# Three edits to a nine-stage layer stack: an unrolled attention stage, experts moved into a gather stage, normalizations spread over three engines

## What is computed

```python
h = h + _L1_attn_ref(_layernorm(h, axis=-1), ...)
h = h + _L1_ffn_ref(_layernorm(h, axis=-1), ...)
...
h = h + _L3_ffn_ref(_layernorm(h, axis=-1), ...)

def _layernorm(x, axis=-1, eps=1e-05):
    m = jnp.mean(x, axis=axis, keepdims=True)
    v = jnp.var(x, axis=axis, keepdims=True)
    return (x - m) / jnp.sqrt(v + eps)
```

```python
a_src = (h * att_src).sum(-1); a_dst = (h * att_dst).sum(-1)
e = jax.nn.leaky_relu(a_src[src] + a_dst[dst], negative_slope=0.2)
... # softmax of e over the edges of each target, weighted sum of h[src]
scores = _layernorm(agg, ln_gamma, ln_beta).reshape(M, HEADS, NUM_EXPERTS).mean(1)
topk_s, topk_i = jax.lax.top_k(scores, TOP_K)
for ei in range(NUM_EXPERTS):
    g = jnp.where(topk_i == ei, w, 0.0).sum(-1)
    hh = jax.nn.gelu(x @ W1[ei] + b1[ei], approximate=False)
    out = out + g[..., None] * (hh @ W2[ei] + b2[ei])
```

## Time and profile before

| | us |
|---|---|
| median of 3 runs (lowest to highest) | 18901.3 (18895.3 to 18918.1) |
| the profiled execution: device time | 18988.5 |
| the profiled execution: span of its trace | 18986.7 |
| busy in that span: PE, DVE, ACT, POOL | 11533, 8751, 5824, 2169 |
| layer 1 attention, sequence 0's first unit to the last result | 2429 to 4599 |
| gather block | 15688 to 18525 |
| gates (`g6`) | 18536 to 18660 |
| experts (`f3`) | 18660 to 18972 |

### The profile page before, as it was taken

One profiled execution on the slowest core, in us unless ns is written; L12 is line 12 of the kernel. 1 busy time (PEld: TensorE's weight loads), 2 busy tenths in 40 slices (PEclk: granted clock), 3 DMA queues, 4 the chain that ended last, 5 costly groups with the idle time before them and its releaser, 6 DMA issues. The chain is left out here.

```text
span 18986.7 us, 169231 instructions
## 1 busy us (share of the span) xinstructions
PE 11533.1 (61%) x41513; PEld 7179.7 (38%) x41513; DVE 8751.2 (46%) x29125; ACT 5823.9 (31%) x13473; POOL 2169.1 (11%) x2242
## 2 busy tenths in 40 slices
PE   2588599998553311139999999999889610000004
PEld 1477466665323300014444444444567500000004
DVE  5544544444312278876666666666422382111102
ACT  1344234443113310025555555555333200000001
POOL 0000000000000000000000000000000007777771
PEclk5566577777656655569999999999755555555555
DMA  0000000000021100014333444334100104222220
GB/s 3 3 0 0 1 4 0 0 0 2 20 88 44 46 6 2 2 42 98 98 98 98 99 99 98 96 98 99 34 0 0 18 0 43 24 20 20 20 15 10
DMA packets 481191, 688.04 MB, mean 36 GB/s; under 512 B 168462, under 2 KB 423015, under 8 KB 460898
## 3 DMA queue, kind: packets, MB, share of 16 engines
q1 hardware_dynamic: 405826, 641.72, 13.6%
q0 software_dynamic: 74592, 38.28, 3.4%
HBM read 405.88 MB, written 83.41 MB: 26 GB/s over the span
## 5 line engine op out<-in xcount | busy, mean ns | idle before, releaser
L1562 PE MATMUL pm_out<-pm_w,pm_tab 128*128 128x484 f32 x8192 | 4009.8, 570 | 0.2 <-DVE pm_w L1727 0.2
L1727 DVE SCALAR_TENSOR_TENSOR pm_w<-pm_sums,pm_e 128x484 f32<-128x484 f32 x4096 | 2647.2, 658 | 1021.2 <-ACT pm_e L1655 977.8
L1655 ACT ACTIVATE pm_e<-pm_sums 128x484 f32<-128x484 f32 x4096 | 2315.7, 573 | 1407.8 <-PE pm_sums L1576 1406.1
L2292 POOL DMA_INDIRECT g_got<-gat_sources,ed_idx x2048 | 1982.8, 968 | 685.7 <-issue 674.5
L1562 PEld LDWEIGHTS pm_out<-pm_w,pm_tab 128*128 128x128 f32 x8192 | 1555.7, 191 | 1039.7 <-DVE pm_w L1727 593.3
L2208 POOL DMA_INDIRECT ed_first<-gat_targets,so_at x1 | 2.9, 2882 | 15674.2 <-DVE so_at L2218 15674.2
L2450 PE MATMUL g_ps<-k_ident,g_wide 128*20 128x128 f32 x3 | 0.8, 409 | 2885.2 <-DVE g_wide L2472 2885.2
L1576 PE MATMUL pm_sums<-pm_mv,pm_pick 96*128 96x484 bf16 x4096 | 1512.9, 370 | 35.9 <-DMA pm_mv<-pm_parts 20.1
L2450 PEld LDWEIGHTS g_ps<-k_ident,g_wide 128*20 128x20 f32 x3 | 0.3, 111 | 2885.5 <-DVE g_wide L2472 2885.4
L2388 DVE TENSOR_TENSOR g_e<-g_got,g_b 128x512 f32<-128x512 f32 x16 | 11.1, 692 | 2039.4 <-DMA g_got<-gat_sources,ed_idx 2039.3
L2327 ACT ACTIVATE g_ex<-g_ex 128x1024 f32<-128x1024 f32 x16 | 16.9, 1056 | 2795.2 <-DVE g_ex L2403 2795.2
(11 more groups left out here) (496 smaller groups left out, 21224.3 us busy)
## 6 DMA issues: line engine op xcount, KB each, us to landing
pm_tab<-in_L_ffn_tables SPq DMA_DIRECT2D x128, 2048.0 KB, 7.7
pm_mv<-pm_parts SPq DMA_DIRECT2D x3072, 60.5 KB, 2.4
qkv_rows<-p_q SPq DMA_DIRECT2D x32, 1452.0 KB
a_qkv<-qkv_rows SPq DMA_DIRECT2D x96, 484.0 KB
g_got<-gat_sources,ed_idx POOLq DMA_INDIRECT x2048, 2.6
pm_gb<-pk_threshold_rows SPq DMA_DIRECT2D x128, 242.0 KB, 7.2
gat_running<-g_rec SPq DMA_DIRECT2D x16, 1536.0 KB, 5.9
gat_heads<-ed_same SPq DMA_DIRECT2D x4, 1024.0 KB
```

The source lines that it names most:

```text
L1562: pe.matmul(out[:, hd % 2, 0:CHUNK], tab[hd % 2][:, t, :], w[:, t % NW, :], start=(t == 0), stop=(t == KT - 1)).then_inc(used, 1)
L1655: a.activation(e[:, t % NW, :], sums[:, t % NB, 0:CHUNK], ACT.Exp).then_inc(exp_ready, 1)
L1727: v.scalar_tensor_tensor(out=w[:, t % NW, :], in0=sums[:, t % NB, 0:CHUNK], scalar=0.0, in1=e[:, t % NW, :], op0=ALU.is_gt, op1=ALU.mult). ...
L2292: g.indirect_dma_start(got[c][:, w, :], None, rows, bass.IndirectOffsetOnAxis(ap=idx[:, i * W + w:i * W + w + 1].bitcast(U32), axis=0)).th ...
```

## The change

1. **Normalization in quarters.** The 64 tiles are cut in four quarters. VectorE subtracts the mean on three of them and GpSimd on the fourth; ScalarE squares all four; VectorE sums the squares quarter by quarter; at the end VectorE scales three quarters and GpSimd the fourth. The semaphores are shared by all nine calls.
2. **Layer 1 attention without a loop.** `samples` writes all 32 sequences out on all engines. TensorE's wait for the last value copy (`v3`) moves from before the first projection of a sequence to the fifth head, and the transpose that prepares the next sequence gets a wait of its own for `v3` of the sequence before.
3. **Experts under the gathers.** The `f3` block is gone. Each of the 16 chunks of the gather block now also computes the experts of two sequences, ahead of the chunk's own work on VectorE and ScalarE, and SyncE stores the results (with bias, not yet weighed) to DRAM. The `got` buffers go from four to three. The `g6` block loads the results back in four pieces as it starts, and weighs, sums and adds them on VectorE in whole pieces of 16 tiles once the gates are there.

```diff
+    QUARTERS = [slice(q * TILES // 4, (q + 1) * TILES // 4) for q in range(4)]
+        centre = lambda e, q: e.tensor_tensor(xn[:, q, :], h[:, q, :], spread(mean[:, q], C), ALU.subtract)
...
-                v.tensor_tensor(xn[:, :, :], h[:, :, :], spread(mean, C), ALU.subtract).then_inc(done, 1)
-                v.wait_ge(done, 3)
-                v.tensor_tensor(sq[:, :, :], xn[:, :, :], xn[:, :, :], ALU.mult).then_inc(done, 1)
-                v.wait_ge(done, 4)
-                v.tensor_reduce(var, sq[:, :, :], AX.X, ALU.add).then_inc(done, 1)
-                v.wait_ge(done, 5)
+                for q in QUARTERS[0:3]:
+                    centre(v, q).then_inc(done, 1)
+                for n, q in enumerate(QUARTERS):
+                    v.wait_ge(root, R + n + 1)
+                    ins = v.tensor_reduce(var[:, q], sq[:, q, :], AX.X, ALU.add)
+                ins.then_inc(done, 1)
...
-                v.tensor_tensor(xn[:, :, :], xn[:, :, :], spread(rstd, C), ALU.mult).then_inc(done, 1)
+                for q in QUARTERS[0:3]:
+                    v.tensor_tensor(xn[:, q, :], xn[:, q, :], spread(rstd[:, q], C), ALU.mult)
+
+            @block.gpsimd
+            def _(g):
+                last = QUARTERS[3]
+                g.wait_ge(done, D + 2)
+                centre(g, last).then_inc(pooled, 1)
+                g.wait_ge(done, D + 8)
+                g.tensor_tensor(xn[:, last, :], xn[:, last, :], spread(rstd[:, last], C), ALU.mult)
             @block.scalar
             def _(a):
-                a.wait_ge(done, 6)
+                for n, q in enumerate(QUARTERS):
+                    if n < 3:
+                        a.wait_ge(done, D + n + 3)
+                    else:
+                        a.wait_ge(pooled, G + 1)
+                    a.activation(sq[:, q, :], xn[:, q, :], ACT.Square).then_inc(root, 1)
+                a.wait_ge(done, D + 7)
                 a.activation(std, var, ACT.Sqrt).then_inc(root, 1)
...
         def samples(eng, first, body, end):
             first()
-            body(0, True, False)
-            with eng.Fori(1, PAIRS - 1) as i:
-                body(i, False, False)
-            body(PAIRS - 1, False, True)
+            for i in range(PAIRS):
+                body(i, i == 0, i == PAIRS - 1)
             end(PAIRS * 2 * NH)
...
                         pe.wait_ge(DV, pd.after(b, "x"))
+                        if b:
+                            pe.wait_ge(AC, pa.after(b - 1, "v3"))
...
-                            if n == 0:
-                                pe.wait_ge(AC, pa.after(b, "v3"))
                             project(u, n, c)
                             if not (lead and n < 1):
                                 score(*ago(1))
+                            if n == 4:
+                                pe.wait_ge(AC, pa.after(b, "v3"))
...
-            W, SLOTS, RING = 128, 4, 4
+            W, SLOTS, RING = 128, 3, 4
...
+                            for l in both:
+                                v.wait_ge(mlp[l], ml.before(i))
+                                v.tensor_copy(xs[l][:, :, :], xn[:, (i * LANES + l) * NT:(i * LANES + l + 1) * NT, :]).then_inc(mlp[l], 1)
+                            for l in both:
+                                v.wait_ge(mlp[l], made(i, "y"))
+                                v.tensor_tensor(y[l][:, :, :], ps[l][0:TP, 3, :].rearrange("p (t n) -> p t n", t=NT), repeat(b2[:, :], NT),
+                                                ALU.add).then_inc(mlp[l], 1)
                             v.wait_ge(head_in[c], 16 * (i // 2 + 1))
...
+                            if i < CHUNKS:
+                                for c in both:
+                                    sp.wait_ge(mlp[c], made(i, "bias"))
+                                    sp.dma_start(expert_rows[:, (i * LANES + c) * NT:(i * LANES + c + 1) * NT, :], y[c][:, :, :]).then_inc(mlp[c], 16)
...
+                    for q in range(PIECES):
+                        sp.dma_start(y[q][:, :, :, :].rearrange("p t e c -> p t (e c)"), expert_rows[:, q * PIECE:(q + 1) * PIECE, :]).then_inc(y_loaded[q], 16)
...
+                    for q in range(PIECES):
+                        tiles = slice(q * PIECE, (q + 1) * PIECE)
+                        v.wait_ge(y_loaded[q], 16)
+                        v.wait_ge(s, after("gates"))
+                        tt(y[q][:, :, :, :], y[q][:, :, :, :], spread(gates[:, tiles, :], C), ALU.mult).then_inc(s, 1)
+                        v.wait_ge(s, after(f"weigh{q}"))
+                        red(red_[q % 2][:, :, :], y[q][:, :, :, :].rearrange("p t e c -> p t c e"), AX.X, ALU.add).then_inc(s, 1)
+                        v.wait_ge(s, after(f"blend{q}"))
+                        tt(h[:, tiles, :], h[:, tiles, :], red_[q % 2][:, :, :], ALU.add).then_inc(s, 1)
```

More of the change, by code:

```diff
@@ L2062, in stage_l3_ffn @@
     heads_at = nc.dram_tensor("gat_heads", (ED + NODES * 128, NHD), F32, kind="Internal").ap()
+    expert_rows = nc.dram_tensor("gat_expert_rows", (TP, TILES, NE * C), F32, kind="Internal").ap()
     running = nc.dram_tensor("gat_running", (ED + 129, REC), F32, kind="Internal").ap()
@@ L2244, in stage_l3_ffn @@
                 two = range(2)
+                CA, HD = C + 1, 2 * C
+                w1, w2, b2 = sb("w1", [CA, NE, HD]), sb("w2", [HD, NE, C]), sb("b2", [TP, NE * C])
+                xs = [sb(f"xs{c}", [TP, NT, C]) for c in both]
+                xT = [sb(f"xT{c}", [CA, T]) for c in both]
+                hid = [sb(f"hid{c}", [HD, NE, T]) for c in both]
+                y = [sb(f"y{c}", [TP, NT, NE * C]) for c in both]
+                ps = [ctx.enter_context(nc.psum_tensor(f"g3_ps{c}", [128, 4, BANK], F32)) for c in both]
+                load_all(nc, ctx, "f3", [
+                    (w1[0:C, :, :], A["L3_ffn_W1"].rearrange("e c n -> c e n")),
+                    (w1[C:CA, :, :].rearrange("p e n -> p (e n)"), row(A["L3_ffn_b1"].rearrange("e n -> (e n)"))),
+                    (w2[:, :, :], A["L3_ffn_W2"].rearrange("e n c -> n e c")),
+                    (b2[:, :], row(A["L3_ffn_b2"].rearrange("e c -> (e c)")).to_broadcast([TP, NE * C]))],
+                    [(xT[c][C:CA, :], 1.0) for c in both])
+                ml = Chain([ctx.enter_context(nc.semaphore(f"g3_mlp_step{c}")) for c in both], ["x", "turn", "xT", "hid", "gelu", "y", "bias", "store:16"])
+                mlp, made = ml.sem, ml.after
                 got = [sb(f"got{c}", [128, W, SRC]) for c in range(SLOTS)]
@@ L2293, in _ @@
                                     ap=idx[:, i * W + w:i * W + w + 1].bitcast(U32), axis=0)).then_inc(gathered[c], 16)
+                    @block.tensor
+                    def _(pe):
+                        for i in range(PAIRS):
+                            for c in both:
+                                pe.wait_ge(mlp[c], made(i, "x"))
+                                pe.transpose(ps[c][:, 0, 0:TP], xs[c][:, :, :].rearrange("p t c -> p (t c)"),
+                                             ident[0:TP, 0:TP]).then_inc(mlp[c], 1)
+                            for c in both:
+                                pe.wait_ge(mlp[c], made(i, "xT"))
+                                for n in range(NE):
+                                    ins = pe.matmul(ps[c][:, 1 + n // 2, (n % 2) * T:(n % 2 + 1) * T], w1[:, n, :], xT[c][:, :], start=True, stop=True)
+                                ins.then_inc(mlp[c], 1)
+                            for c in both:
+                                pe.wait_ge(mlp[c], made(i, "gelu"))
+                                for t in range(NT):
+                                    for n in range(NE):
+                                        ins = pe.matmul(ps[c][0:TP, 3, (t * NE + n) * C:(t * NE + n + 1) * C], hid[c][:, n, t * TP:(t + 1) * TP],
+                                                        w2[:, n, :], start=True, stop=True)
+                                ins.then_inc(mlp[c], 1)
                     @block.sync
@@ L2324, in _ @@
                         for i in range(CHUNKS):
+                            for c in both:
+                                a.wait_ge(mlp[c], made(i, "turn"))
+                                for t in range(NT):
+                                    ins = a.activation(xT[c][0:C, t * TP:(t + 1) * TP], ps[c][t * C:(t + 1) * C, 0, 0:TP], ACT.Copy)
+                                ins.then_inc(mlp[c], 1)
+                            for c in both:
+                                a.wait_ge(mlp[c], made(i, "hid"))
+                                a.activation(hid[c][:, :, :].rearrange("p (k n) w -> p k (n w)", k=2), ps[c][:, 1:3, 0:2 * T], ACT.Gelu).then_inc(mlp[c], 1)
                             c = i % 2
@@ L2503, in stage_l3_ffn @@
             ag = sb("ag", [TP, TILES, REC])
+            PIECES = 4
+            PIECE = TILES // PIECES
+            y = [sb(f"y{q}", [TP, PIECE, NE, C]) for q in range(PIECES)]
+            red_ = [sb(f"red{q}", [TP, PIECE, C]) for q in range(2)]
```

(3 more changed lines are left out.)

103 lines of the change are left out of this document (20 added, 83 removed).

## The result

The changed kernel takes 18274.7 us (median of 4 runs, 18262.7 to 18290.3). The kernel before takes 18898.3 us (4 runs, 18857.3 to 18918.1). The ratio is 0.967, interval 0.966 to 0.969: 624 us less, where 452 were forecast.

The account below looks back on a forecast made before the run. TensorE at a low clock was taken to bound layer 1's attention, GpSimd's gathers the program's end, then the experts alone. Gains of 170 + 34 + 248 = 452 us took 18901 to about 18450 us, range 18260 to 18640.

Parts of the forecast that it names:

- Part 1: Layer 1's attention written out without a loop: 170 us gained, range 90 to 300.
- The sign of being right: Layer 1's attention: the stretch from first to last result of 28 sequences would be near 1730 us.
- I take 12 falls: Layer 1's attention: 12 long clock falls at ninth heads in 28 sequences, costing 235 of 406 us.
- Both bounds of it, 7 and 14 of 28: Layer 1's attention: ninth-head falls from 5 of 20 seen, or alternating sequences; gains of 259 or 132 us.
- Part 2: Nine normalizations in quarters: 3.75 us gained each, 34 us in all, ends -3 to 54.
- the order of turns: Normalization: GpSimd starts its quarter after VectorE's three, at 3.5 us, and ends at 5.8, in time.
- The price of 2.3 us: Normalization: GpSimd's arithmetic on one quarter, taken midway by ratio between 1.23 and 4.42 us.
- Part 3: Experts moved under the gathers at the program's end: 248 us gained, range 205 to 255.
- The second: Rival, layer 1's attention: the clock stays up and all 406 us come, 18213 us; chance 0.09.
- The first: Rival, layer 1's attention: the ninth head takes over all falls, gain 0 to 90 us, 18575 us; chance 0.20.
- The third: Rival, layer 1's attention: written-out lists starve for instructions, 672 us lost there, 19290 us; chance 0.06.
- the fourth: Rival, last stage: experts slow the gathers, 0.05 us each taking 100 us of the gain, 18550 us; chance 0.07.

Follow-up runs that it names:

- the second run: The changed kernel once more, no edit: 18494.1 us against 19142.4 for the kernel before on its chip, ratio 0.966.
- the last run: Changed kernel with layer 1's square root and reciprocal on VectorE, k steps one head later, norms' last quarter on VectorE: 18466.5 us, ratio to the kernel before 0.964.
- the sweep: Layer 1's attention written out, wait moved, with b extra products in head 4 of sequence b: layer 1's attention took 1863.7 us.
- the first four runs: On one chip: kernel before again 19140 us; against its 19118.1 median, the attention change alone 18757.3, norms alone 19122.9, experts alone 18900.6.

## Why the prediction was right, and where it was not

The time, 18274.7, lies in the range, 15 us above its lower end and 175 under the forecast. The two profiled executions are 716 us apart, which is what the parts below add up to; the medians are 624 apart, since the profiled execution before stood 90 us over its median. That it does is in part luck. The best ends of the three parts, 300, 54 and 255, lead to 18292, and the time is below that. The recorded lower end of 18260 had 32 us more, for which the working names no term, and part 1 alone was outside its own range.

**Part 1 was mis-sized, 170 against 395 in the same 28 sequences.** The sign of being right, 1730 us for them, was missed by as much: 1505. Right were the cause at the loop end, that the ninth-head stall would stay, that the clock would fall only there, and that the moved wait gives nothing. Wrong was the term "I take 12 falls": there were none of that length, in the trace of the second run one. Both bounds of it, 7 and 14 of 28, were counts of ninth-head falls in the looped stage, where VectorE's branch stands between them. They were no bounds for a stage without it. Five long falls of 20 stalls before, one of some 140 after. The range of 90 to 300 left out what came, 438 us between the two traces, 361 in the run of this part alone and 413 with the wait kept. Brief falls, which the working had only in passing at about 10 us, are all that is left, and cost 16.

**Part 2** was forecast at 34 us and is 26 by the trace. The step that failed is the order of turns: I let GpSimd start behind VectorE's third quarter, but it came before the second, and VectorE waited. From the subtraction to the end of the sum of squares the gain is 3.7 us and not 5.15, and the last step loses 0.8 us and not 1.4. The price of 2.3 us is not tested, since the 2.94 us can hold a wait. The Trainium skill (GPSIMD Engine Reference, Engine selection) advises against elementwise work on GpSimd; the last run agrees: without it the norm is 1.1 us shorter.

**Part 3** was right: 251 us alone, 254 between the two traces less the norm, against 248. The strided sum took 7.08 us (7.5 assumed; the upper figure of 1.9 ns an element should have been 1.97, that is 1.01 us over 512, which gives 8.1 and not 7.9 us), and the gathers were lengthened by 5 us at most.

**The rivals.** The second, the clock stays up (18213, chance 0.09), came nearest to what happened in the attention, and I had given it too little. What I had put against it were the five long falls at the ninth head, some of them two sequences after the last loop end. Of the five traces with all lists written out four have no such fall, which fits that they need the loop's rhythm, but the fifth has one. The first, all falls at the ninth head, has the place right and the length wrong. The third did not come: no VectorE step in the written-out attention waits 3 us for nothing. Nor did the fourth.

**Open.** What decides between a fall of 4 and of over 40 us. It is not the length of the stall alone: stalls of 1.0 us and stalls of 1.8 to 2.1 us both had long falls, brief ones and none behind them. The run with the doubled transposition shows that the spacing of the stalls changes the pattern of the falls; that it also decides their length fits the sweep and the run with VectorE alone written out, but is argued.

## What to carry to other kernels

Where a matmul-bound stage is paced by TensorE and its clock is under 1.0, look for the short waits in front of each fall, and price a stall of 1 to 2 us by the half-clock time that follows, not by itself. A count of falls taken in the old rhythm is no bound for the new one; let the range reach to none and to all. Take the loop off the engine whose product TensorE waits for, first VectorE here, and then the last stall too, since only the stage without any had the same time for each sequence.

## What the runs showed of the hardware

- A taken branch at the end of a long loop body held VectorE for 2.95 us and TensorE behind it for 2.01 us. TensorE's own branch made no wait of 0.9 us or more. The Trainium skill (Runtime: NRT & Kernel Launch, Instruction fetch mechanics) has a stall for a taken branch whose target lies outside the window, and gives TensorE a larger instruction memory than most engines; that this tells the two apart here no run shows.
- Executions of one kernel differed by 0.9% (19040 to 19204 us, 17 runs) on one chip, and the looped stage by 72 us among four traces; with layer 1's loops away the executions differed by 0.1% (18744 to 18761, 4 runs).
- A GpSimd product of 1024 elements on two SBUF inputs lasted 2.94 us beside VectorE, whose own take 1.2 us, and VectorE's next one ended 1.8 us late.
- Chips differ in the gathers: mean 968 or 969 ns on the first and on one of the other three, 1044 to 1054 on the remaining two; the last stage of the kernel before was 3974 us on the first and 4175 on that of the first four runs.
